# TensorE turns both units of a pair in one step and clears two banks there; counts of the first body use two halves of a bank

## The reference, cut to what matters

```python
h  = relu(layernorm(x)); xn = layernorm(h) * ln_w + ln_b
w_phys   = (silu(rbf @ w1 + b1) @ w2 + b2) * cutoff[:, None]      # one row an edge
msg_phys = xn[col] * w_phys
q_e, k_e, v_e = (xn @ wq + bq)[row], (xn @ wk + bk)[col], (xn @ wv + bv)[col]
scores   = sum(q_e * k_e, per head) / sqrt(32) * cutoff
attn     = softmax(scores over the 8 heads)
combined = msg_phys + gate * attn * v_e
aggr     = segment_sum(combined, row, num_segments=n)
out      = x + h + aggr @ wo + bo
```

## Time and profile before

| | us |
|---|---|
| median of 3 runs (lowest, highest) | 5246.67 (5241.54, 5255.47) |
| the profiled execution, its span | 5255.2, 5253.5 |
| TensorE busy | 5005.0 (95%) |
| VectorE, ScalarE, GpSimd busy | 4025.0, 3923.5, 3747.6 |
| body 0 of prep | 149.8 to 381.6 |
| the rest of prep | to 2590 |
| edges, with query chunks still loading | 2590 to 2765 |
| edges, steady | 2765 to 5130 |
| finish | to 5253.5 |

### The profile page before, as it was taken

The page is one execution under the profiler, slowest core; times in us unless marked ns, Lnnn a source line. Parts: engine busy times, 40 slices in busy tenths (PEclk is TensorE's granted clock), DMA queues, the critical chain, the costliest instruction groups (busy, mean ns, idle before and its releaser), DMA issues. The chain is left out here.

```text
span 5253.5 us, 116799 instructions
## 1 busy us (share of the span) xinstructions
PE 5005.0 (95%) x24352; PEld 3893.1 (74%) x24353; DVE 4025.0 (77%) x7424; ACT 3923.5 (75%) x12601; POOL 3747.6 (71%) x3476
## 2 busy tenths in 40 slices
PE   3879999999999999999679999999999999999999
PEld 2556666666676666667468888888888888888887
DVE  9789996676665556532368999999999999999994
ACT  4445566666666666656569999999999999999993
POOL 1557777777777777777657777777777777777770
PEclk9989999999999999999889999999999999999999
DMA  6233444444454344444499999999999999999956
GB/s 204 89 105 111 164 157 140 160 158 145 149 172 158 134 165 156 135 157 156 174 333 358 367 364 368 367 363 365 365 369 367 367 368 368 363 368 367 370 200 198
DMA packets 584400, 1306.16 MB, mean 249 GB/s; under 512 B 81246, under 2 KB 384134, under 8 KB 582961
## 3 DMA queue, kind: packets, MB, share of 16 engines
q0 software_dynamic: 221536, 881.08, 44.4%
q1 hardware_dynamic: 311796, 345.48, 21.6%
q10 hardware_dynamic: 50850, 77.03, 4.0%
HBM read 1024.15 MB, written 324.38 MB: 257 GB/s over the span
## 5 line engine op out<-in xcount | busy, mean ns | idle before, releaser
L1031 POOL DMA_INDIRECT ukvx<-kvx_table,urec x1760 | 1937.3, 1101 | 594.2 <-issue 560.1
L341 POOL DMA_INDIRECT records<-rows,slot_i x1660 | 1742.9, 1050 | 686.8 <-issue 469.0
L696 PE MATMUL w_ps<-w2s,hid 128*128 128x256 f32 x6656 | 1554.9, 387 | 51.1 <-DVE rows L610 50.9
L696 PEld LDWEIGHTS w_ps<-w2s,hid 128*128 128x128 f32 x6656 | 1250.5, 193 | 375.9 <-issue 156.9
L610 DVE TENSOR_TENSOR rows<-w_ps,b2b 128x512 f32<-128x512 f32 x832 | 571.4, 687 | 746.8 <-PE w_ps L696 746.6
L810 ACT ACTIVATE hid<-hid_ps,b1t 128x512 f32<-128x512 f32 x832 | 525.4, 682 | 823.0 <-PE hid_ps L685 808.4
L1134 PE MATMUL uq_ps<-aggr,uonehotT 128*128 x3520 | 982.8, 402 | 0.8 <-issue 0.5
L1154 PE MATMUL ag_ps<-ukvx,uonehot 128*128 128x256 f32 x3520 | 908.3, 381 | 0.0
L1159 PE MATMUL ag_ps<-ukvx,uonehot 128*128 128x256 f32 x3520 | 905.8, 380 | 0.0
L1218 DVE TENSOR_TENSOR ukvx<-uq_ps,ukvx 128x512 f32<-128x512 f32 x880 | 604.9, 687 | 224.3 <-PE uq_ps L1134 224.3
L831 ACT ACTIVATE rows<-rows 128x256 f32<-128x256 f32 x1664 | 706.9, 504 | 66.3 <-DVE rows L610 66.1
(11 more groups left out here) (175 smaller groups left out, 5085.9 us busy)
## 6 DMA issues: line engine op xcount, KB each, us to landing
urec<-records SPq DMA_DIRECT2D x880, 260.0 KB
rbf_in<-in_edge_attr SPq DMA_DIRECT2D x207, 256.0 KB, 2.9
kvx_table<-kvx ACTq DMA_DIRECT2D x10, 3456.0 KB, 14.5
ukvx<-kvx_table,urec POOLq DMA_INDIRECT x1760
records<-rows,slot_i POOLq DMA_INDIRECT x1661, 2.1
records<-kvx SPq DMA_DIRECT2D x1, 13000.0 KB
aggr<-query_table SPq DMA_DIRECT2D x7, 1792.0 KB, 20.8
fbase<-x_plus_h SPq DMA_DIRECT2D x14, 896.0 KB, 7.0
```

What stands on the lines that cost most here:

```text
L341: pool.indirect_dma_start(recs, bass.IndirectOffsetOnAxis(ap=slot_i[:, q, t:t + 1], axis=0), rows[:, q, t, :], None).then_inc(scattered[q] ...
L696: m = pe.matmul(w_ps[j % 2][:, h, :], hid[:, k % 2, c, h, j * P:(j + 1) * P], w2s[:, c, :], start=(h == 0 and c == 0), stop=(c == 1), skip ...
L1031: pool.indirect_dma_start(kvx[:, k, j, :], None, table, bass.IndirectOffsetOnAxis(ap=rec[:, k, j, R_DST:R_DST + 1].bitcast(I32), axis=0), ...
```

## The change

Five edits belong together in edges. The turn of the even unit u+3 and that of the odd unit u+4 both stand in TensorE's odd step, where `turn_ps` now has room for two units; even steps have no turn. The two clearings of a pair stand there too, and wait for the `keep` of the odd unit itself (`u + 1`) where each waited for the one before. ScalarE's odd step runs `keep` ahead of `spread` and `pick`. Spread and pick run one unit further ahead (`SPREAD_AHEAD` 6), as turns come a step earlier. The copying out of an even unit waits for both turns. In prep, buckets counted in body 0 use two halves of the bank in turn, and a bucket is settled after the next one has been counted.

```diff
+            def counts(chunk, nth):
+                at = nth % 2 * (TMAX // 2) if chunk == 1 else 0
+                return cs_ps[:, at:at + T]
...
             def count_up(b, m, chunk, nth):
+                behind = 1 if chunk == 1 else 0
                 dve.wait_ge(s["compared"], nth + 1)
-                    dve.wait_ge(s["settled"], nth)
+                    dve.wait_ge(s["settled"], nth - behind)
...
             def settle(b, m, chunk, nth):
+                if chunk == 1 and nth > 0:
+                    dve.wait_ge(s["settled"], nth)
...
+                        if chunk == 1:
+                            count_up(own + mine[j], j, chunk, done + mine[j])
+                            if j:
+                                settle(own + mine[j - 1], j - 1, chunk, done + mine[j - 1])
+                            continue
...
+                    if chunk == 1:
+                        for m in range(4, len(mine)):
+                            count_up(own + mine[m], m, chunk, done + mine[m])
+                            settle(own + mine[m - 1], m - 1, chunk, done + mine[m - 1])
+                        settle(own + mine[-1], len(mine) - 1, chunk, done + mine[-1])
...
-        GATHER_AHEAD, SPREAD_AHEAD, TURN_AHEAD, OUT_AHEAD, ASK_AHEAD = 6, 5, 3, 2, 2
+        GATHER_AHEAD, SPREAD_AHEAD, TURN_AHEAD, OUT_AHEAD, ASK_AHEAD = 6, 6, 3, 2, 2
...
             def evacuate(u, k, i, first):
-                act.wait_ge(s["turned"], u + 1)
+                act.wait_ge(s["turned"], u + 2 - k % 2)
...
                 if k % 2 == 0:
                     behind(exponent, 1, u, k, i, first)
+                elif not (first and k < LAG):
+                    keep(u - LAG, bucket_of[2])
                 ahead(spread, SPREAD_AHEAD, u, k, i, first, last)
                 ahead(pick, SPREAD_AHEAD - 1, u, k, i, first, last)
-                if not (first and k < LAG):
-                    keep(u - LAG, bucket_of[k % 2 * 2])
+                if k % 2 == 0 and not (first and k < LAG):
+                    keep(u - LAG, bucket_of[0])
...
             def renew_next(u, last_bucket):
-                if not (isinstance(u, int) and u == 0):
-                    pe.wait_ge(s["kept"], u)
-                renew(sums(last_bucket + 2, SUMS - 2, 1, RENEW))
+                pe.wait_ge(s["kept"], u + 1)
+                for ahead_by in (2, 4):
+                    renew(sums(last_bucket + ahead_by, SUMS - 2, 1, RENEW))
...
-                ahead(turn, TURN_AHEAD, u, k, i, first, last)
-                if not (first and k < LAG):
-                    renew_next(u - LAG, summed[half + 1])
+                if k % 2:
+                    ahead(turn, TURN_AHEAD, u, k, i, first, last)
+                    ahead(turn, TURN_AHEAD + 1, u, k, i, first, last)
+                    if not (first and k < LAG):
+                        renew_next(u - LAG, summed[half + 1])
```

More of the change, by code:

```diff
@@ L435, in compare @@
                 dve.tensor_scalar(eq[:, m, 0:T], bucket[:, c0:c0 + T], ids[:, bass.ds(b, 1)], None, ALU.is_equal).then_inc(s["compared"], 1)
+            def counts(chunk, nth):
+                lo, hi = CHUNKS[chunk]
+                T = (hi - lo) * BODY * GC
+                at = nth % 2 * (TMAX // 2) if chunk == 1 else 0
+                return cs_ps[:, at:at + T]
             def count_up(b, m, chunk, nth):
@@ L439, in count_up @@
                 T = (hi - lo) * BODY * GC
+                behind = 1 if chunk == 1 else 0
                 dve.wait_ge(s["compared"], nth + 1)
-                if not (isinstance(nth, int) and nth == 0):
-                    dve.wait_ge(s["settled"], nth)
-                dve.tensor_tensor_scan(cs_ps[:, 0:T], eq[:, m, 0:T], eq[:, m, 0:T], run[:, bass.ds(b, 1)], ALU.add, ALU.max).then_inc(s["scanned"], 1)
+                if not (isinstance(nth, int) and nth <= behind):
+                    dve.wait_ge(s["settled"], nth - behind)
+                dve.tensor_tensor_scan(counts(chunk, nth), eq[:, m, 0:T], eq[:, m, 0:T], run[:, bass.ds(b, 1)], ALU.add, ALU.max).then_inc(s["scanned"], 1)
             def settle(b, m, chunk, nth):
@@ L614, in body @@
                             count_up(own + mine[j], j, chunk, done + mine[j])
-                    for m in range(3, len(mine)):
+                    if chunk == 1:
[3 more added lines that the diff above has]
+                        settle(own + mine[-1], len(mine) - 1, chunk, done + mine[-1])
+                    for m in range(3, len(mine) if chunk != 1 else 3):
                         if m > 3:
@@ L1089, in _ @@
             act.wait_ge(s["one_ready"], 1)
-            for k in range(SPREAD_AHEAD):
+            for k in range(PICKS):
                 spread(k, k, 0, True)
@@ L1096, in _ @@
                 widen(k, k, 0, True)
+            for k in range(PICKS, SPREAD_AHEAD):
+                spread(k, k, 0, True)
+                pick(k - 1, k - 1, 0, True)
             def unit(u, k, i, first, last):
@@ L1122, in turn @@
                 pe.wait_ge(s["picked"], u + 1)
-                if not (first and k == 0):
+                if k % 2 == 0 and not (first and k == 0):
                     pe.wait_ge(s["ohT_ready"], u)
                 for j in range(2):
-                    m = pe.transpose(turn_ps[:, j, :], ohb[:, k % PICKS, j, :], ident_bf[:])
+                    m = pe.transpose(turn_ps[:, k % 2 * 2 + j, :], ohb[:, k % PICKS, j, :], ident_bf[:])
                 m.then_inc(s["turned"], 1)
@@ L1160, in aggregate @@
                 m.then_inc(s["ag_done"], 1)
-            for k in range(TURN_AHEAD):
+            for k in range(TURN_AHEAD + 1):
                 turn(k, k, 0, True)
@@ L1205, in _ @@
                 aggregate(UNITS - LAG + n, DEPTH - LAG + n, summed[half:half + 2])
-                if n + 1 < LAG:
+                if n % 2 and n + 1 < LAG:
                     renew_next(UNITS - LAG + n, summed[half + 1])
```

9 lines of the change are left out of this document (6 added, 3 removed).

## The result

The median of six runs is 5270.2 us (5266.1 to 5276.1), beside 5247.4 for six runs of the kernel before: a ratio of 1.0039, 95% interval 1.0027 to 1.005, so 14 to 26 us slower. The forecast was 5256, with 5216 to 5284 around it. The profiled execution took 5272.35 us, its span 5270.6, which is 17.1 more than the span before. The kernel before was run again beside each group of experiments: 5248.5 us beside e1 to e4, 5251.3 beside e5 to e8, 5252.0 beside e9 to e11, 5251.4 beside e12. Ratios are to these, so that a difference in us from the kernel after carries up to 5 us of that drift.

What follows compares the result with a forecast made beforehand. TensorE's own instructions were taken to bound steady edges, where it works without a break. Body 0 -19, steady edges +15 and the query-chunk stage +13 sum to +9 us on 5246.7: 5256 us, range 5216 to 5284.

Steps and rivals of the forecast that it cites:

- The wait for `keep`: Steady edges: clearings waiting for the odd unit's `keep` delay the next sums, losing 0.45 us a round against 0.28 saved.
- just fits: Steady edges, plain pair: TensorE's sequencer has the sums' addresses ready at 3521.05, weights wanted at 3521.07; no loss.
- stands 0.45 us in one pair of five: Steady edges, end of a loop round: the branch makes the sequencer late and TensorE idles 0.45 us before the sums.
- stays as it is: Steady edges, ScalarE: everything up to the odd step's widening at 3518.33 is unchanged, so `keep` is done at 3519.21.
- second rival: Steady edges: the wait for `keep` is late in every pair by a further 0.1 us; +34 more, 5290; chance 0.10.
- The saving: Steady edges: transposes and clearings grouped per pair take 0.385 against 0.44 us; 0.055 saved a pair, 23 us in 420 pairs.
- A full weight load for the second clearing: Steady edges, rival: the second clearing's weights cost a full 0.11 us, so 23 us are not saved; 5274, chance 0.06.
- The query stage: Stage with query chunks: four waits for records each grow by 2.8 to 3.7 us, 11 to 15 us; +13 taken.
- 8 to 9: Stage with query chunks, expected sign: TensorE idle 8 to 9 us at the four waits for records, where 5.5 was.
- Body 0: Prep's body 0: counting ahead shortens a group of six buckets by 1.14 us; sixteen groups make -19 us.
- Met in time everywhere: Steady edges, rival: the wait for `keep` is met in time everywhere; -29 in all, 5218; chance 0.28.
- The other two: Rivals: second clearing's weights cost a full 0.11 us (5274, chance 0.06); counting in halves brings nothing in body 0 (5275, 0.06).

Runs made afterwards that it cites:

- e1: Kernel before with only the edits of the first body's counts, edges as they were: 5233.4 us, ratio 0.9962.
- e4: Kernel after with the odd step's clearings and their wait moved behind the odd query's four passes: 5233.3 us, ratio 0.9968.
- e5: Kernel after with ScalarE's odd-step copy to SBUF (`keep`) ahead of the widening: 5268.2 us, ratio 1.0031.
- e8: Kernel after with TensorE's bank numbers worked out ahead of its wait and ScalarE's copy ahead of the widening: 5225.4 us, ratio 0.9945.
- e9: Kernel after with ScalarE's copy ahead of the widening and the copy's addresses worked out ahead of its wait: 5243.2 us, ratio 0.9982.
- e11: Kernel after with the odd unit's `keep` put back behind `spread` and `pick`: 5457.6 us, ratio 1.0384.
- e12: Kernel before with only `spread` six units ahead instead of five, and its start-up: 5264.5 us, ratio 1.0026.
- e3: Kernel after with the bank numbers of both clearings worked out ahead of TensorE's wait for `keep`: 5230.6 us, ratio 0.9964.
- e10: Kernel after with bank numbers and copy addresses ahead of their waits, copy ahead of widening, query chunks in four parts: 5206.8 us, ratio 0.9906.
- e2: Kernel before with all edits except those of the first body's counts: 5284.7 us, ratio 1.0066.

## Why the prediction was right

Its cause, its signs and its three places hold. Its size does not hold as well: +9 was forecast, and it came out at +17.1 in the traces and at 14 to 26 in the runs. By the table, body 0 gave 14.1 and not 19, the edges lost 18.0 and not 15, the query stage 12.1 and not 13, and the finish 1.0 where nothing was put. Two of these came out as near as they did by luck, as shown below.

**The wait for `keep`.** The step on which the forecast rested was that a plain pair "just fits" and TensorE "stands 0.45 us in one pair of five". Measured: some 0.055 in three plain pairs of five (0.03 to 0.07), none in the pair behind a late one, 0.48 at the loop's end (6.02 less 5.54). e3, e4, e9 and e11 show that this is the length from `keep` to the sums: where the sums wait for it, it stayed at 1.95 (e11) and 2.45 (e9 and e11) when the copy was moved, and at the loop's end it fell to 2.06 when register work was taken from behind the wait. The time followed each time. The branch that the forecast blamed for the loop's end stands in the sequencer's rows with 0.50 us. "Just fits" was right for the first sums of a plain pair and 0.05 us off for the second; 0.055 in three pairs of five is 0.165 a round, 14 us in 84 rounds, and is a part of the edges' term that the forecast did not have. The step behind it is that on ScalarE everything up to the odd widening "stays as it is": that puts the end of `keep` 4.64 us behind the turn (3519.21 less 3514.57), and it came at 4.76 (loop's end) to 4.87, for one because the evacuation, which now waits for both turns, starts 0.11 later. That is the lateness of the second rival. It cost 14 us and not the 34 named there, and in e9, with the copy 0.2 to 0.3 us earlier, no plain pair is late.

The record of an instruction that waits doesn't show its wait: the register instruction (L1164) at 3522.7 is 32 to 36 ns long and comes as its semaphore does. The Trainium skill (Perfetto Trace Analysis, Sequencer-only Instruction) says the same, that the record covers the execution alone; so the loss appears as "issue" at the sums two microseconds on.

**The saving.** Undisturbed pairs went from 5.627 to 5.540, 0.087 and not 0.055: the two clearings and the step to the query take 0.055 in all (3529.22 to 3529.28), where 0.055 + 0.03 was put. Five pairs save 0.43 a round and lose 0.64, 0.21 net, and 84 rounds make 17.6; the table has 18.0 where +15 was forecast. Two errors nearly cancelled: 13 us too little saved (0.032 on 420 pairs) and 14 us too little lost in plain pairs; that this term is near is luck. A full weight load for the second clearing had been a rival: the clearing stands less than 0.03 behind the first with a load of its own. The Trainium skill (TensorE: Matmul & The Clock Gate, LDWEIGHTS) has a load take its columns divided by 1.2, an estimate of 107 ns for 128 columns. The trace comes near that in the length of a record (98 ns for a clearing's load) but not in the pace, since the loads overlap.

**The query stage.** +13 forecast, +12.1 measured. The idle time before the turn grew to 5.8 to 7.5 us, not to the "8 to 9" named as the sign: the step of 2.8 to 3.7 per wait is too large. At the four records TensorE's wait grew by 0.3 (12.5 to 12.8), 1.7, 1.1 and 2.8, 5.9 in all, and this is half of the stage's growth; so the sum came near by luck. e12 shows that the earlier spread is the cause of 7.5 us of the term; the rest is open.

**Body 0.** Groups of six fell from 11.71 to 10.50, 1.21 against 1.14 forecast, and the body from 231.8 to 211.6, -20 against -19. At the end of prep 14.1 of it was left in this trace, and by ten traces with the new counts against three with the old 15.5 (means 2552.9 and 2568.4); e1's median is 15 below 5248.5. So the term looks 3 to 5 us too large. Up to the last addition of body 0 the gain was there, 19.9 us (351.1 against 371.0); behind it 5.8 were lost, and 5 of them are three body starts at the lower clock that this trace has and that of the kernel before has not (last section). Whether the counts cost the bodies behind them anything is not shown.

**The rivals.** "Met in time everywhere" is close to what e10 does: it needed `keep` some 0.2 us earlier and 0.4 us less behind the wait. "Late in every pair" holds in part, in three plain pairs of five and at half the size. The other two fell: the second clearing cost under 0.03 and not 0.11, and the counts brought some 15 us.

## What to carry to other kernels

Where an engine's sequencer waits ahead of address work, count from the release to the first instruction that the engine needs, not to the instruction that waits; here 1.95 us, and 2.45 across a loop's end, made a wait late that was met a microsecond before the array came to it (`keep` ends at 3528.17, the clearings run at 3529.22). Working out addresses ahead of such a wait added no instruction and was worth 33 us in the pairs (e3). And before a producer is moved forward, look whether it waits in the same way (e5), and over how many rounds its chain closes (e11).

## What the runs showed of the hardware that was not expected

TensorE's clock at a body's start. In three kernels the same sixteen passes behind about the same idle time:

```profile
952.30 3.79 PE L696 MATMUL w_ps<-w2s,hid 128*128 128x256 f32 x16 [2.01 <-DVE rows L610]
```

```profile
932.12 5.41 PE L716 MATMUL w_ps<-w2s,hid 128*128 128x256 f32 x16 [2.10 <-DVE rows L620]
```

```profile
1136.53 5.41 PE L696 MATMUL w_ps<-w2s,hid 128*128 128x256 f32 x16 [1.93 <-DVE rows L610]
```

The first is the kernel before, the second the kernel after, the third e12, with the old counts. The granted clock over the 5.5 us of the second is 0.69, over the 3.8 of the first 1.00, so that it was at the lower level (1.2 GHz) for part of it. It costs 1.6 us each time. Of the three body starts looked at in every trace (those of the groups 64, 80 and 96), none, two and two were slow in the three traces with the old counts (before, e2, e12), and one to three in the ten with the new; both kinds have it, and it can move prep by some 5 us from one execution to the next. It does not explain e2, whose prep is 7.9 us shorter than before with two slow starts more. There 7.3 us are won by the last addition of body 0 already (363.7 against 371.0), and the granted clock over the first 380 us is 0.95 against 0.93; by that share alone, an estimate, it would be 0.02 of 380 us, 7.6. What decides either was not found.
